# A mixture-of-experts layer on one core: the experts' up half as 7 block products on 2048 sorted tokens each

## The reference

```python
# x: 2 x 2048 x 512; N = 4096 tokens, D = 512, H = 2048, two experts
ys = cond / sqrt(512)
d  = rsqrt((ys*ys) @ (W*W) + 1e-8)
xf = ((x * ys) @ W) * d                         # the projection: 4096 x 512
top1 = argmax(softmax(xf @ gate_w.T))           # one expert of two for each token
masked = xf * one_hot(top1)                     # for each expert e
h   = relu(masked @ w1[e] + b1[e])              # "up":   512 -> 2048
y_e = h @ w2[e] + b2[e]                         # "down": 2048 -> 512
shared = relu(xf @ sw1 + sb1) @ sw2 + sb2       # the shared part, for all tokens
out = x + y_0 + y_1 + shared
```

## Time and profile before

| | |
|---|---|
| time, median of 3 | 1421.04 us |
| time of the profiled execution | 1422.55 us |
| its span | 1420.0 us |
| PE busy | 1413.4 us |
| DVE busy | 846.7 us |
| ACT busy | 503.1 us |
| POOL busy | 312.8 us |
| moved by DMA | 215.66 MB |

### The profile page before, as it was taken

One profiled execution on the slowest core, in us unless ns is written; L12 is line 12 of the kernel. 1 busy time (PEld: TensorE's weight loads), 2 busy tenths in 40 slices (PEclk: granted clock), 3 DMA queues, 4 the chain that ended last, 5 costly groups with the idle time before them and its releaser, 6 DMA issues.

```text
span 1420.0 us, 17714 instructions
## 1 busy us (share of the span) xinstructions
PE 1413.4 (100%) x6262; PEld 1172.7 (83%) x6262; DVE 846.7 (60%) x1362; ACT 503.1 (35%) x776; POOL 312.8 (22%) x354
## 2 busy tenths in 40 slices
PE   9999999999999999999999999999999999999998
PEld 8888888888888888888888888888888888888886
DVE  7979968868898878786755314143264522424225
ACT  4456644445564444445432211111142211111112
POOL 0000000044113300000140613406134051431533
PEclk9999999999999999999999999999999999999999
DMA  6967485766899979786763301203035130220212
GB/s 200 298 209 232 168 260 185 251 212 225 290 288 304 302 265 275 265 252 222 215 191 107 74 20 28 48 13 68 20 91 164 30 69 19 49 41 7 63 22 34
DMA packets 157702, 215.66 MB, mean 152 GB/s; under 512 B 46560, under 2 KB 68576, under 8 KB 157632
## 3 DMA queue, kind: packets, MB, share of 16 engines
q1 hardware_dynamic: 142752, 186.71, 41.1%
q0 software_dynamic: 14880, 28.07, 9.5%
HBM read 131.19 MB, written 85.75 MB: 153 GB/s over the span
## 4 chain that ended last, share of the span: by engine, by line
PE 97%; DVE 1%; issue 1%; POOL 0%; DMA 0%; POOLq 0%; DVEq 0%
PE bank L2009 24%; PE bank L2033 24%; PE bank L1974 21%; PE bank L1937 20%; PE bank L1865 6%; PE bank L2029 1%; PE bank L1842 0%; PE bank L1848 0%; POOL out L785 0%; DVE rows L1301 0%; DMA out<-res,tab 0%; POOL out L788 0%; DVE res L1764 0%; DVE vb L1370 0%; DVE vt L1352 0%
## 5 line engine op out<-in xcount | busy, mean ns | idle before, releaser
L1738 DVE CAST h_hi<-hf 128x512 fp32r<-128x512 f32 (+1 forms) x128 | 57.2, 447 | 386.4 <-ACT hf L1093 348.5
L1093 ACT ACTIVATE hf<-bank,b 128x512 f32<-128x512 f32 (+1 forms) x128 | 87.2, 681 | 546.7 <-PE bank L2009 479.6
L1937 PE MATMUL bank<-xw,w_hi 128*128 128x512 f32 x896 | 276.1, 390 | 0.2 <-DVE vb L1370 0.2
L1974 PE MATMUL bank<-hl,w_hi 128*128 128x512 f32 x896 | 276.1, 389 | 0.0
L768 POOL DMA_INDIRECT rows_e<-xf_scratch,soft x144 | 143.1, 994 | 599.0 <-DVE xe_lo L1611 249.5
L2009 PE MATMUL bank<-xe_lo,w_hi 128*128 128x512 f32 (+1 forms) x512 | 197.8, 386 | 0.0
L2009 PE MATMUL bank<-xe_hi,w_hi 128*128 128x512 f32 (+1 forms) x512 | 197.8, 386 | 0.0
L1937 PEld LDWEIGHTS bank<-xw,w_hi 128*128 128x128 f32 x896 | 168.1, 188 | 35.5 <-DVE vb L1370 0.7
L1974 PEld LDWEIGHTS bank<-hl,w_hi 128*128 128x128 f32 x896 | 168.2, 188 | 35.2 <-DVE hl L1337 0.3
L2009 PE MATMUL bank<-xe_hi,w_lo 128*128 128x512 f32 (+1 forms) x512 | 196.2, 386 | 0.0
L2033 PE MATMUL bank<-w_hi,h_lo 128*128 128x512 f32 x496 | 193.2, 389 | 0.0
(11 more groups left out here) (227 smaller groups left out, 1700.5 us busy)
## 6 DMA issues: line engine op xcount, KB each, us to landing
hin<-hidden_scratch SPq DMA_DIRECT2D x112, 512.0 KB, 4.9
hidden_scratch<-vb SPq DMA_DIRECT2D x80, 512.0 KB, 4.0
hidden_scratch<-vt SPq DMA_DIRECT2D x32, 512.0 KB, 3.8
stage<-w_pack SPq DMA_DIRECT2D x64, 256.0 KB, 2.9
ring<-x_cols SPq DMA_DIRECT2D x32, 256.0 KB, 4.8
xf_scratch<-xo SPq DMA_DIRECT2D x32, 256.0 KB, 4.5
rows<-xf_scratch SPq DMA_DIRECT2D x16, 512.0 KB, 7.6
aux<-w_pack SPq DMA_DIRECT2D x16, 512.0 KB, 6.4
```

Source lines behind the costliest of these rows:

```text
L1093: nc.scalar.activation(hf[:, j % 2, 0:width(u)], hidden_bank(j, first and e > 0)[:, 0:width(u)], ACT.Relu, bias=b1[:, 1 + e, j:j + 1]).the ...
L1738: nc.vector.tensor_copy(h_hi[:, buf, 0:filled_n], hf[:, j % 2, 0:filled_n]).then_inc(hh_ready, 4)
L1937: last = nc.tensor.matmul(up_bank(u, UP_BANK[c])[p][:], w[:, DOWN_W[c], pair, part], xw[:, c, x, k, :], start=(c in FRESH and n == 1), sto ...
L1974: last = nc.tensor.matmul(bank[p][:], w[:, DOWN_W[c], i, part], hl[:, n % HL, h, :], start=(i == 0 and q == 0), stop=(i == PAIRS - 1 and q ...
```

## The change

- The experts' up half becomes 4 more blocks of stage 2's own groups (s = 4 to 7, u = 16 to 31; `UPS` = 8), each on 1024 sorted tokens. Each expert gets exactly 2048 places (`CAP`). Its results go to DRAM plainly (`expert_hidden`), without the four sums; ScalarE makes the relu of a third piece (`b12_made`).
- The weights for it are loaded and split pair by pair, in groups 14, 16, 17, 18 and 22, 24, 25, 26 (`RAW_JOBS`), those of the shared down half in 29 to 31.
- The tokens must lie sorted in DRAM for that: POOL gathers 48 tiles of 128 rows by the table into one of two buffers and stores them to `sorted_scratch` (`sort_in`, `sort_out`), from group 10. `next_rows` waits for 8, 16, 40 and 48 of these tiles.
- The experts' down half follows the shared one as plain products on pieces loaded back from `expert_hidden` (`expert_unit`), with all down weights resident: 8 wides of 512 tokens x 16 x 4 x 3 matmuls.
- What an expert has beyond 2048 tokens goes in units of 64, now called loose: their up half in a counted loop behind groups 20 and 28 (`loose_up`), their down half in a counted loop ahead of wide 3 (`loose_down`), and their rows in 16 more tiles at the end of the scatters.

In the diff, the first `loose_up` is ScalarE's and the second TensorE's.

```diff
-FIRST = T - S
+UPS = 2 * BLOCKS
+GU = GROUPS * UPS
+CAP = N // 2
+UNITS_E = N // T
+COLS = NT + CAP // P
-PLACE_GROUP = 8
-SCATTER_GROUP = 9
-TABLE_GROUP = 14
+SCATTER_GROUP = 6
+SORT_GROUP = 10
+SORT = (*range(KD * W), *range(NT, COLS), *range(KD * W, NT))
+LOOSE_UP = ((BLOCKS + 1) * GROUPS, (UPS - 1) * GROUPS)
+LOOSE_DOWN = 3
...
             def next_rows(s, q):
                 sp.wait_ge(xw_lo, STEPS * (s + 1))
+                if s + 1 >= BLOCKS and q == 0:
+                    tiles_done = SORT.index(W * 2 * (s + 2 - BLOCKS) - 1) + 1
+                    sp.wait_ge(sorted_out[0], DMA * (tiles_done // 2))
+                    sp.wait_ge(sorted_out[1], DMA * (tiles_done // 2))
+                if s * GROUPS == LOOSE_UP[0] and q == 0:
+                    sp.wait_ge(loose_up_done, 2)
...
             for c in range(NT):
-                pool.wait_ge(up_mm, PER_GROUP * SCATTER_GROUP + 2 * c)
+                pool.wait_ge(up_mm, PER_GROUP * SCATTER_GROUP + 3 * c // 2)
...
+            def sort_in(k):
+                pool.wait_ge(up_mm, PER_GROUP * SORT_GROUP + 2 * k)
+                wait(pool, sorted_out[k % 2], DMA * (k // 2))
+                u = SORT[k]
+                pool.indirect_dma_start(sorted_rows[k % 2][:], None, xf_rows,
+                                        bass.IndirectOffsetOnAxis(tab_in[:, u:u + 1], 0)).then_inc(sorted_in[k % 2], DMA)
+            def sort_out(k):
+                pool.wait_ge(sorted_in[k % 2], DMA * (k // 2 + 1))
+                pool.dma_start(sorted_tile(SORT[k]), sorted_rows[k % 2][:]).then_inc(sorted_out[k % 2], DMA)
+            for k in range(COLS):
+                sort_in(k)
+                if k > 0:
+                    sort_out(k - 1)
+            sort_out(COLS - 1)
...
+            def loose_up(e, x):
+                for q in range(QUADS):
+                    act.wait_ge(loose_clear, e + 1)
+                    act.wait_ge(loose_mm, QUADS * x + q + 1)
+                    nc.scalar.copy(hq[0:S, q, :], loose_banks[q][0:S, :]).then_inc(loose_flat, 1)
+                act.wait_ge(loose_lo, 2 * x + 2)
+                loose_rows_load(x + 1)
+                for q in range(QUADS):
+                    act.wait_ge(loose_back, QUADS * x + q + 1)
+                    for i in range(4):
+                        j = 4 * q + i
+                        nc.scalar.activation(hu[:, j, :], loose_turned[q % 2][:, i * P:i * P + S], ACT.Relu,
+                                             bias=b1[:, 1 + e, j:j + 1]).then_inc(loose_relu, 1)
+                act.wait_ge(loose_relu, HC * (x + 1))
+                act.dma_start(loose_unit(x), hu[:]).then_inc(loose_kept, DMA)
+                act.dma_start(loose_unit(x + 1), hu[:]).then_inc(loose_kept, DMA)
+                loose_rows_hi(x + 1)
+                act.wait_ge(loose_kept, 2 * DMA * (x + 1))
...
+            def loose_up(u, x):
+                pe.wait_ge(loose_lo, 2 * x + 2)
+                for q in range(QUADS):
+                    if q == 0:
+                        pe.wait_ge(up_added, 6 * (u + 1))
+                        pe.wait_ge(up_kept, 8 * (u + 1))
+                    pairs = slice(W * (q % 2), W * (q % 2) + W)
+                    terms = ((0, 0), (2, 2)) if q < 2 else ((0, 1), (KD, 3))
+                    for n, (kk, slot) in enumerate(terms):
+                        for k in range(2):
+                            for i, w in enumerate((w8_hi, w8_lo)):
+                                last = nc.tensor.matmul(loose_banks[q][:], xu[:, kk + k, :, :], w[:, slot, pairs, k * P:(k + 1) * P],
+                                                        start=(n == 0 and k == 0 and i == 0), stop=(n == 1 and k == 1 and i == 1))
+                    last.then_inc(loose_mm, 1)
+                for q in range(QUADS):
+                    pe.wait_ge(loose_folded, QUADS * x + q + 1)
+                    if q > 1:
+                        pe.wait_ge(loose_relu, HC * x + 4 * (q - 1))
+                    for i in range(4):
+                        part = slice(i * P, (i + 1) * P)
+                        last = nc.tensor.transpose(loose_turned[q % 2][:, part], hq[:, q, part], ident[:])
+                    last.then_inc(loose_back, 1)
+                pe.wait_ge(loose_relu, HC * (x + 1))
...
+            def expert_unit(v, j, tiles):
+                e, n = v // (UNITS_E // 2), E_UNITS + HC * v + j
+                pe.wait_ge(hu_lo, n + 1)
+                pe.wait_ge(we_lo, 2 * (W * e + j // W) + j % W // 2 + 1)
+                for m in tiles:
+                    if j == 0:
+                        if v < 2:
+                            pe.wait_ge(dn_added, 14 * (BLOCKS - 1) + (6, 10)[m // 2] if v == 0 else 14 * BLOCKS)
+                        else:
+                            pe.wait_ge(out_ready, W * (v - 2) + m + 1)
+                    part = slice(m * P, (m + 1) * P)
+                    for q, (h, w) in enumerate(((0, w8_hi), (0, w8_lo), (1, w8_hi))):
+                        last = nc.tensor.matmul(y_bank(v, m)[:], hl[:, n % HL, h, part], we_tile(w, e, j),
+                                                start=(j == 0 and q == 0), stop=(j == HC - 1 and q == 2))
+                    if j == HC - 1 and m < W - 1:
+                        last.then_inc(y_mm, 1)
+                return last
+            def loose_down(e, x):
+                bank = y_bank(LOOSE_DOWN, 0)
+                pe.wait_ge(out_ready, W * (LOOSE_DOWN - 2) + 1)
+                pe.wait_ge(hv_lo, 2 * x + 2)
+                for j in range(HC):
+                    half = hv_halves[j // PAIRS]
+                    last = nc.tensor.matmul(bank[:], half[:, j % PAIRS, :, :], we_tile(w8_hi, e, j), start=(j == 0), stop=(j == HC - 1))
+                last.then_inc(loose_y_mm, 1)
+                for j in range(HC):
+                    half = hv_halves[j // PAIRS]
+                    nc.tensor.matmul(bank[0:S, :], half[:, j % PAIRS, 0, :], we_tile(w8_lo, e, j), start=False, stop=(j == HC - 1),
+                                     skip_group_check=True).then_inc(loose_y_mm, 1)
+                pe.wait_ge(loose_sum, 2 * x + 2)
```

More of the change, by code:

```diff
@@ L58 @@
 JH = T // B32
-JN = T // B32
-JU = P // B32
+JU = S // B32
 FLIPS = 4
@@ L845, in _ @@
[L845 to L861 removed]
+            pool.wait_ge(tab_dma, 2 * DMA)
@@ L966, in up_group @@
                 jobs = RAW_JOBS.get(u, ())
-                last = u == GROUPS * BLOCKS - 1
-                more = g == GROUPS - 1 and s < BLOCKS - 1
+                last = u == GU - 1
+                more = g == GROUPS - 1 and s < UPS - 1
+                shared = s < BLOCKS
                 def take(dst, c, h, f):
@@ new lines, in _ @@
+            spilled = []
+            for s in range(UPS):
+                for g in range(GROUPS):
+                    u = GROUPS * s + g
+                    if u == LOOSE_UP[0] and not spilled:
+                        for i in range(2):
+                            act.wait_ge(sorted_out[i], DMA * ((SORT.index(COLS - 1) + 1) // 2))
+                        act.wait_ge(pick_ready, 1)
+                        act.wait_ge(loose_filled, 2 * DMA)
+                        loose_rows_load(0)
+                    up_group(s, g)
+                    if u in LOOSE_UP:
+                        e = LOOSE_UP.index(u)
+                        if e == 0:
+                            spilled = read_split(act)
+                            loose_rows_hi(0)
+                        with act.If(spilled[e] > 0):
+                            with act.Fori(0, spilled[e]) as x:
+                                loose_up(e, x)
+                        act.wait_ge(loose_clear, e + 1)
+                        nc.scalar.copy(primed[:], ones[:, 0:1]).then_inc(loose_up_done, 1)
@@ L1836, in _ @@
+            for m in range(W):
+                take_rows(UNITS_E - 1, m)
         @block.tensor
@@ L2037, in wide_slot @@
-            def wide_slot(u, e, first=False):
-                if first:
-                    for j, passes in ((0, (0, 1)), (1, (0, 1)), (0, (2,)), (2, (0, 1)), (1, (2,)), (2, (2,))):
-                        hidden(u, e, j, passes, True)
-                for j in range(HC):
-                    if not first or j > 2:
-                        hidden(u, e, j)
-                    if j >= 2 and j < HC - 1:
-                        down(u, e, j - 2)
-                down(u, e, HC - 3)
-                down(u, e, HC - 2)
-                down(u, e, HC - 1)
```

1097 lines of the change are left out of this document (452 added, 645 removed).

## The result

The changed kernel takes 1460.47 us (median of 4 runs, 1454.93 to 1471.43) where the kernel before takes 1420.97: a ratio of 1.0285, 95% interval [1.0258, 1.0313]. It is slower by 39.5 us; the prediction was 1397 us, 24 us faster. The profiled execution is the longest of the four, 1471.43 us with a span of 1469.7, so what its trace shows as lost is 11 us more than the median lost.

What follows compares the result with a forecast made beforehand. TensorE was taken as the bound, 97% of the chain. Matmuls 1362.6, loose unit 16.1 and 8.2, tail 7.0 make 1393.9 us, 26.1 less; 1421.04 - 26.1 + 2 for the sort gives 1397, forecast 1393 to 1401, range 1391 to 1408.

Steps and rivals of the forecast that it cites:

- the tail: Behind the last matmul: one bank's addition, POOL's start, an adding scatter to its landing, drain and end, 7.0 us.
- The matmuls: Experts' up 304.8 us, shared down 305.8, experts' down 348.1; from stage 2's end at 403.86 they reach 1362.6 us.
- the loose unit: Tokens beyond 2048: up part behind group 28 costs 16.1 us, down part ahead of wide 3 costs 8.2.
- their sum: Whole span without a charge for the sort: 1362.6 + 16.1 + 8.2 + 7.0 = 1393.9 us against 1420.0.
- the charge for lateness: Behind the loose up part, ScalarE's stores and the held-back down weights make things late: 1.5 us, ends 0 and 4.
- Rival 3: Granted clock falls in the loose part, so following matmuls run at 1.2 GHz: 2.4 us to twice that, 1399 to 1402; chance 0.14.
- What must be hidden: the sort: Up stages: gathers start near 302, 5.2 us a tile, 40th tile at 510 against about 512; 2 us charged.
- My own bound: Sort's store landing at 6.1 us, seen at DMA share 1.00: period 7.4, 40th tile at 598, 86 us late.
- more room: Waits for 8, 16 and 32 sorted tiles: 344 against 343 and free behind it, 385 against 419, 468 against 480.
- The sort's load on others: During the sort: it adds some 0.3 of DMA load, and POOL's and SyncE's streams slow each other; no separate charge.
- Rival 2: Slower: sort's landing above 4.8 us, period 6.1, 40th tile 34 us late, 30 us lost, 1425; chance 0.06.

Runs made afterwards that it cites:

- experiments 1: Changed kernel reading unsorted rows, without the waits for sorted tiles: 1416.43 us; with the sort's gathers and stores left out too: 1404.04 us.
- experiment 3: Changed kernel with four steps of POOL's chain of loose rows run ahead, while it waits for the next output tile: 1453.05 us.
- experiment 7: Changed kernel without the sort and all waits for it, and with POOL's chain of loose rows four steps ahead: 1396.26 us.
- Experiment 2: Changed kernel with only ScalarE's wait for 32 sorted tiles taken away, its 64-token units reading the unsorted copy: 1459.41 us.
- the slowed version: Changed kernel with three sort buffers, early table writes, loose-row chain ahead, 12 sort tiles at once and the rest 4 matmul counts apart: 1411.52 us.

## Why the prediction was wrong, by its own steps

The kernels of experiments 1, 3 and 7 divide the 64.2 us between 1396.3 and 1460.5: 7.8 for the tail (7.4 in experiment 3), 12.4 for the sort's transfers, 44.0 for the waits on it. The 44.0 is the part that carries the changed kernel's spread.

- **The matmuls, the loose unit and their sum: right.** 1393.9 us of span was forecast without the sort, 1394.1 measured in experiment 7, where the shared down half begins at 723.8 (I had said near 725). That it fits within 0.2 us is in part luck: the loose up part came 1.8 us shorter than the 16.1 charged, while the clock cost 1.6 and the tail 0.7 more. The up stages run at 19.05 us a group. The loose up part is 14.3 us (717.4 to 731.7) against 14.6 without the charge for lateness; ScalarE's issues, for which I had no row and took 0.47 us, are 0.45 (four loads in 1.79 us). The loose down part is 8.6 against 8.2.
- **Rival 3, the clock in the loose part: it happened.** Its price was 2.4 us and up; in 731.66:740 the granted clock is 0.67, and 8.34 x 0.33 = 2.8 us. In experiment 7 it is 0.56 for 3.6 us, so 1.6 us, below that price. The sum hardly shows it, since I had charged 1.5 us for what is late, and nothing was. TensorE was idle for 3.6 us beside the transposes there, and no run tells the one's part in the fall from the other's.
- **"What must be hidden: the sort" failed; this is the step that made the prediction wrong.** The start was right (302, measured 302.1). The period was not, though its steps were the right ones: I had one gather's issue with a gap, 1.3, and one landing, 3.9. Both were too small. The landing is 4.9 as a mean; and the gather's issue, 1.18, begins 0.76 behind the landing it waits for, together 1.9 where I had 1.3. That is 6.8, and 6.72 over all 48. The landing is the larger part of the error, and for a period that adds up over 40 tiles the mean counts, not the median (4.4). 1.5 us too little 40 times is 60 us: the 40th tile landed at 573 instead of 510. My own bound (a landing of 6.1, 598) held it, and I gave that side 0.06 and stopped the pricing at 34 us late.
- **The other waits were not free.** I gave the 8, 16 and 32 tiles "more room". At 6.7 us a tile the 8th and the 32nd came too late. Experiment 2 shows that the 32nd was still no cost of its own, but the 8th had a side that I hadn't looked at: stores queued behind SyncE's wait. The rule that a wait is to be costed by what is queued behind it applies to SyncE's stores too, and they hold ScalarE.
- **The sort's load on others was costed at nothing.** I used the DMA share to price the sort's landing, and never the landing of the 512 KB stores that TensorE depends on through ScalarE. That is 12.4 us.
- **The tail: half the step was missing.** The 7.0 us were right for a last scatter that starts when its tile is ready (7.6 in experiment 3). But POOL had 16 tiles of loose rows between the scatters, and I never laid its steps of 9.3 to 11.8 us against TensorE's 10.9 us a tile. That is the 7.4 to 7.8 us.
- **Rival 2 named the right place and the right sign**, with 1425. Priced with the measured period it would have been 1397 - 2 + 59 for the 63 us late less 4 of slack, 1454 us, near the 1460 that came.

What stays open: of the 15.3 us between the slowed version and experiment 7, the 6.7 and 2.0 us waits at 374 and 392 are seen in its trace, and the lower clock behind them; no run kept the copy's traffic away from 350 to 375 without making a later tile late; and no run moved SyncE's stores ahead of its weight and row loads in 350 to 370, which would tell whether the order of the queue or the full DMA engines hold them.

## What to carry to other kernels

A background copy with two buffers has a period of every step round its loop: the landing as a mean under the load that the copy itself adds, the time from the landing to the next issue, and that issue. Look up from where a landing is counted, so that nothing is missing or counted twice. Multiply an error in the period by the number of tiles before you call it small, and give the far bound of the landing a chance of its own. Where several waits hang on one producer, they need not add: here taking away the longest wait of the list gave 1 us, within the noise. And traffic that nobody waits for still has a price: look for the store or load of the bound engine's neighbours that lands later because of it.

## What the runs showed of the hardware

A third buffer raised the median landing of the first 30 stores of 256 KB from 4.7 to 5.8 us and still cut their distance from 7.1 to 4.4 us: here more transfers in flight paid although each became slower. The read of 3072 four-byte numbers out of 64-byte rows took 9.8 and 6.3 us in one place, and 12.2 and 9.0 us when it began 10.6 us earlier, under a DMA share of 0.97 instead of 0.88. The granted clock was 0.84 in 531:600, behind idle times of TensorE (31.9 us before 531, 13.6 us within), so here the stalls cost more than their length: of the 65.6 us lost in 355 to 600, 8.9 are matmuls that took longer.
